# Heads' attentions: first-pass products placed by a pattern, maxima turned a step later, GpSimd storing and loading its own pieces

## What is computed

```python
q = (x_norm @ Wq + bq).reshape(B, T, H, d)     # B, T, D = 4, 512, 256; H, d = 16, 16
k = (context @ Wk + bk).reshape(B, S, H, d)    # S = 1601
v = (context @ Wv + bv).reshape(B, S, H, d)
scores = einsum('bthd,bshd->bhts', q, k) * scale      # layer 2: rotary tables on q and k; layers 2, 3: mask
attn = softmax(scores, axis=-1)
x = x + tanh(g) * (einsum('bhts,bshd->bthd', attn, v).reshape(B, T, D) @ Wo + bo)
```

## Time and the page of the profile before

| | |
|---|---|
| three runs | 3853.88, 3861.94, 3851.54 us (median 3853.88) |
| span of the profiled execution | 3829.6 us |
| median less span | 24.3 us |
| TensorE products busy | 3401.9 us (89%) |
| VectorE, ScalarE, GpSimd busy | 2159.4 (56%), 2034.7 (53%), 745.3 us (19%) |
| longest chain, shares | PE 67%, DVE 13%, DMA 8%, ACT 4%, POOL 3%, issue 3% |

### The profile page before, as it was taken

How to read it: one execution, slowest core, us unless ns; L and a number is a source line. 1 busy time by engine, 2 the same in 40 slices (tenths; PEclk the granted TensorE clock), 3 DMA queues, 4 the chain that set the end, 5 groups by cost and what they waited for, 6 DMA issues and landing times.

```text
span 3829.6 us, 52360 instructions
## 1 busy us (share of the span) xinstructions
PE 3401.9 (89%) x18396; PEld 1770.7 (46%) x18396; DVE 2159.4 (56%) x3463; ACT 2034.7 (53%) x4490; POOL 745.3 (19%) x768
## 2 busy tenths in 40 slices
PE   5899999988689989997899799989987979987997
PEld 3333333325432323332697322323326956687996
DVE  6767676736757777873402477767743033264333
ACT  2566666763236666775333266667772322244664
POOL 2211111003635331000302141210002010022332
PEclk8999999999779999998899799999998989999998
DMA  8132424105664443211874655644208521042554
GB/s 194 42 103 61 106 57 110 26 14 187 178 182 124 101 111 82 45 24 46 267 231 154 185 152 118 171 112 103 77 10 285 186 78 69 1 143 92 184 186 167
DMA packets 314686, 456.02 MB, mean 119 GB/s; under 512 B 66315, under 2 KB 234195, under 8 KB 312251
## 3 DMA queue, kind: packets, MB, share of 16 engines
q1 hardware_dynamic: 233206, 285.70, 27.5%
q0 software_dynamic: 29568, 104.65, 8.2%
q10 hardware_dynamic: 51653, 62.32, 5.8%
HBM read 292.46 MB, written 153.91 MB: 117 GB/s over the span
## 4 chain that ended last, share of the span: by engine, by line
PE 67%; DVE 13%; DMA 8%; ACT 4%; POOL 3%; issue 3%; SPq 1%; ACTq 0%; another core or an unknown queue 0%; POOLq 0%; DVEq 0%
PE pv L1325 14%; PE m L1289 11%; PE s L1311 9%; DVE mxp L1172 9%; PE h L2811 5%; PE y L2819 5%; PE h L2385 4%; PE y L2394 4%; PE y L1791 2%; PE s L1771 2%; PE s L1256 2%; DMA sums<-rc 2%; ACT e_t L1403 1%; DMA ot<-sums 1%; PE m L1333 1%
## 5 line engine op out<-in xcount | busy, mean ns | idle before, releaser
L1172 DVE TENSOR_REDUCE mxp<-m 128x1 f32<-128x802 f32 x1536 | 1447.8, 987 | 526.9 <-PE m L1289 523.2
L1403 ACT ACTIVATE e_t<-s 128x512 f32<-128x512 f32 (+1 forms) x2496 | 1340.3, 599 | 552.0 <-PE s L1311 532.9
L1289 PE MATMUL m<-kaug,qaug 97*128 97x401 bf16 x3072 | 811.6, 347 | 97.5 <-DVE mxp L1172 51.6
L1311 PE MATMUL s<-qaug,kaug 100*128 100x512 bf16 (+1 forms) x2496 | 859.4, 386 | 34.1 <-ACT e_t L1403 29.0
L1325 PE MATMUL pv<-e_t,v 128*32 128x512 f32 (+1 forms) x4992 | 670.3, 609 | 0.2
L1311 PEld LDWEIGHTS s<-qaug,kaug 100*128 100x128 bf16 (+1 forms) x2496 | 229.4, 99 | 733.8 <-ACT e_t L1403 519.6
L1289 PEld LDWEIGHTS m<-kaug,qaug 97*128 97x128 bf16 x3072 | 273.4, 99 | 506.7 <-DVE mxp L1172 265.2
L127 POOL TENSOR_TENSOR rstd<-rstd,mhalf 128x16 f32<-128x16 f32 (+2 forms) x9 | 24.2, 2690 | 1150.8 <-DVE rstd L120 1150.8
L2881 ACT ACTIVATE ez<-h,b 128x128 f32<-128x128 f32 x440 | 120.1, 388 | 159.7 <-PE h L2811 159.7
L1325 PEld LDWEIGHTS pv<-e_t,v 128*32 128x32 f32 (+1 forms) x4992 | 98.6, 108 | 214.9 <-ACT e_t L1403 161.3
L2272 DVE SCALAR_TENSOR_TENSOR y<-y,b 128x256 f32<-128x256 f32 x39 | 16.6, 425 | 303.0 <-PE y L2394 303.0
(11 more groups left out here) (377 smaller groups left out, 3616.2 us busy)
## 6 DMA issues: line engine op xcount, KB each, us to landing
w<-in_L_w POOLq DMA_DIRECT2D x78, 1024.0 KB, 5.4
w<-in_L_w SPq DMA_DIRECT2D x24, 1024.0 KB, 12.7
xregion<-zero ACTq DMA_DIRECT2D x10, 2056.0 KB, 12.2
kaug<-kparts SPq DMA_DIRECT2D x16, 1200.8 KB
kaug<-kready SPq DMA_DIRECT2D x32, 600.4 KB
kaug<-kready SPq DMA_DIRECT2D x16, 1200.8 KB
vn<-values SPq DMA_DIRECT2D x8, 1536.0 KB
values<-p_vb ACTq DMA_DIRECT2D x21, 512.0 KB
```

The costliest lines, as they stand in the source:

```text
L1172: dve.tensor_reduce(a.mxp[:, u.g % 2, half, n:n + 1], a.m_slot[u.m % 2][:].rearrange("p (a n) -> p a n", a=2)[:, :, 0:PIECE + 1], AX.XY, A ...
L1289: m = pe.matmul(slot[:, 512 * k:512 * k + PIECE + 1], a.qaug[0:R_MAX, u.g, j, P * qc:P * qc + P], a.kaug[0:R_MAX, u.g, j, k0:k0 + PIECE + ...
L1311: pe.matmul(slot[0:KW[u.k], :], a.kaug[0:R_ALL, u.g, u.j, P * u.k:P * u.k + KW[u.k]], a.qaug[0:R_ALL, u.g, u.j, :], start=True, stop=True) ...
L1403: act.activation(a.e_t[0:KW[u.k], e % 2, u.j, :], a.s_slot[u.s % 3][0:KW[u.k], :], ACT.Exp).then_inc(s_free.sem, 1)
```

## The change

Three parts. (1) A call's `max` units are placed by a table: `counts[k]` says how many step k gets, `ORDER` where they stand among the four `s2` (S) of the step. Every layer leads by 6 maxima. (2) `peak` directly follows the 32nd `max`; the `turn` is laid out at the end of the next step, ahead of that step's `pv`. (3) Pieces that GpSimd splits (all in the second and third layer but the first one, batches 1 to 3 in the first) are stored by GpSimd's own queue, and GpSimd also loads the key pieces, two pieces ahead. SyncE no longer waits for them in order; a fetch waits for the stores' semaphores.

```diff
-MAX_STEPS = 2 * HG * QC + 2
+MAXIMA = 2 * HG * QC
+LEAD = 6
+FEW = (3, 2, 3, 2, 3, 2, 3, 2, 3, 3, 1, 2, 3)
+MANY = (4, 4, 3, 4, 3, 4, 3, 4, 3, 1, 1, 2, 2)
+ORDER = ("SSSS", "SMSSS", "SMSMSS", "MSSMSSM", "MSMSMSSM")
...
-        self.lead = 8 if mask else 12
...
-    def maxima(self, g, b, begin=0, end=2 * HG * QC + 2, alone=False):
+    def maxima(self, g, b, begin=0, end=MAXIMA):
+        for i in range(begin, end):
             self.add("max", b=b, g=g, k=i)
-            if self.to_turn:
-                self.add("turn", **self.to_turn.pop())
-            yield
-        if end > 2 * HG * QC:
-            self.add("peak", b=b, g=g)
...
+            if i == MAXIMA - 1:
+                self.add("peak", b=b, g=g)
                 self.to_turn.append(dict(b=b, g=g))
             yield
+
+    def turn(self):
+        if self.to_turn:
+            self.add("turn", **self.to_turn.pop())
...
-    def attend(self, g, b, *work):
+    def attend(self, g, b, peaks, counts, *work):
         given = [0] * len(work)
         for k in range(KT):
-            for j in range(HG):
+            turning, j = bool(self.to_turn), 0
+            for it in ORDER[counts[k]]:
+                if it == "M":
+                    next(peaks, None)
+                    continue
                 self.add("s2", b=b, g=g, k=k, j=j)
                 n = HG * k + j
+                j += 1
...
+            if turning:
+                self.turn()
             if self.late:
                 self.add("pv", **self.late.pop())
...
+def head_stores_itself(a, u):
+    return u.by == "pool" and (a.ready or u.b > 0)
+
+def head_store_pool(kn, a, u):
+    pool, done, stored = kn.nc.gpsimd, kn.sema("split_pool"), kn.sema(f"pooled{u.f}", DMA)
...
+    pool.wait_ge(done.sem, done.at(u.n + 1))
+    store_parts(pool, u.kind, dst, a.split_at[u.f][2][:, :, 0:n], stored.sem)
+
+def head_load_pool(kn, a, x):
...
+    pool.dma_start(kf[:, 0:n], src).then_inc(arrived.sem, DMA)
+    for r in (0, P // 2) if rope else ():
+        pool.dma_start(kr[r:r + P // 2, 0:n], src[P // 2 - r:P - r, :]).then_inc(arrived.sem, DMA)
...
-            sp.wait_ge(split[u.by].sem, split[u.by].at(u.n + 1))
-            store_parts(sp, u.kind, dst[P * u.j:P * u.j + P, :, c0:c0 + n], a.split_at[u.f][2][:, :, 0:n], stored[u.f].sem)
+            if not head_stores_itself(a, u):
+                sp.wait_ge(split[u.by].sem, split[u.by].at(u.n + 1))
+                store_parts(sp, u.kind, dst[P * u.j:P * u.j + P, :, c0:c0 + n], a.split_at[u.f][2][:, :, 0:n], stored[u.f].sem)
...
             head_split(kn, a, u, pool, "pool")
+            if head_stores_itself(a, u):
+                head_store_pool(kn, a, u)
+            for x in splits[splits.index(u) + 2:][0:1] if a.ready else ():
+                if x.kind == "k":
+                    head_load_pool(kn, a, x)
```

More of the change, by code:

```diff
@@ L577, in lay_out @@
     def lay_out(self):
-        lead, self.late = self.lead, []
+        lead, self.late = LEAD, []
         if self.ready:
@@ L603, in lay_out @@
         v = self.project(0, (), "v")
-        for n, _ in enumerate(self.maxima(0, 0, alone=True)):
+        for n, _ in enumerate(self.maxima(0, 0)):
             if n % 2:
                 next(v, None)
+        self.turn()
         for _ in v:
@@ L634, in lay_out_ready @@
     def lay_out_ready(self):
-        lead = self.lead
+        lead = LEAD
         self.add("begin", b=0)
@@ L646, in lay_out_ready @@
         self.add("prep", k=0)
-        for _ in self.maxima(0, 0, alone=True):
+        for _ in self.maxima(0, 0):
             pass
+        self.turn()
         self.add("prep", k=1)
@@ L870, in head_sp @@
             for f in range(4):
-                if a.dmas.get(f"stored{f}"):
-                    sp.wait_ge(stored[f].sem, stored[f].at(a.dmas[f"stored{f}"]))
+                for name in (f"stored{f}", f"pooled{f}"):
+                    if a.dmas.get(name):
+                        sp.wait_ge(sig(name, DMA).sem, sig(name, DMA).at(a.dmas[name]))
             if u.b:
@@ L932, in head_ready_sp, with store @@
     piece = lambda t: t.rearrange("(c t h i) s k -> c t h i s k", c=DC, t=2, h=H // DC)
-    splits = [x for x in plan.units if x.kind in ("q", "k")]
-    held = []
-    def store():
-        if held:
-            x = held.pop()
+    def store(x):
+        if not head_stores_itself(a, x):
             (c0, n), to = (CHUNKS[x.k], keys) if x.kind == "k" else ((0, T), queries)
@@ L942, in store @@
             store_parts(sp, x.kind, to[x.b, P * x.j:P * x.j + P, :, c0:c0 + n], a.split_at[x.f][2][:, :, 0:n], stored[x.f].sem)
-            head_stored(a, x)
-    def load(x):
-        arrived, (c0, n) = sig(f"kl{x.f}", DMA), CHUNKS[x.k]
-        kf, kr, _ = a.split_at[x.f]
-        if rope and "tables_k" not in a.dmas:
-            left_values()
-            sp.dma_start(a.turn_k[:], a.rope[1]).then_inc(tables_k.sem, DMA)
-            n_of("tables_k")
-        src = kn.dram["keys"][x.b, P * x.j:P * x.j + P, c0:c0 + n]
-        if x.b in LEFT:
-            for f in range(a.p.RING):
-                kept = sig(f"p_k{f}", DMA)
-                sp.wait_ge(kept.sem, kept.at(a.p.stores[f]))
-        sp.dma_start(kf[:, 0:n], src).then_inc(arrived.sem, DMA)
-        for r in (0, P // 2) if rope else ():
-            sp.dma_start(kr[r:r + P // 2, 0:n], src[P // 2 - r:P - r, :]).then_inc(arrived.sem, DMA)
-        for _ in range(a.key_loads):
-            n_of(f"kl{x.f}")
+        head_stored(a, x)
     def left_values():
@@ L1001, in head_ready_sp @@
         elif u.kind in ("q", "k"):
-            store()
-            held.append(u)
-            after = splits[splits.index(u) + 1:][0:1]
-            for x in after:
-                if x.kind == "k":
-                    load(x)
+            store(u)
         elif u.kind == "fetch":
@@ L1010, in head_ready_sp @@
             if "q" in u.what:
-                store()
                 for f in range(2):
-                    last = max(n for (_, b, *_), (at, _, n) in a.stored_of.items() if b == u.b and at == f)
-                    sp.wait_ge(stored[f].sem, stored[f].at(last))
+                    for name in (f"stored{f}", f"pooled{f}"):
+                        of_b = [n for (_, b, *_), (at, n, _) in a.stored_of.items() if b == u.b and at == name]
+                        if of_b:
+                            sp.wait_ge(sig(name, DMA).sem, sig(name, DMA).at(max(of_b)))
             if u.b:
@@ L1084, in head_split @@
         kn.settle(eng, own, eng.tensor_tensor(src, src, a.mask[1][:, u.b:u.b + 1].to_broadcast([P, n]), ALU.mult))
-    before = a.stored_of[u.kind, u.b, u.k, u.j][1]
+    before = a.stored_of[u.kind, u.b, u.k, u.j][2]
     if before:
-        eng.wait_ge(stored.sem, stored.at(before))
+        stored = kn.sema(before[0], DMA)
+        eng.wait_ge(stored.sem, stored.at(before[1]))
     split3(kn, eng, own, kn.cst["ones"][:, 0:1].to_broadcast([P, n]), o, src, [ks[:, k, 0:n] for k in range(3)],
@@ L1094, in head_pool @@
     filled, b_made, biased = kn.sema("filled"), kn.sema("b_made"), kn.sema("biased")
+    splits = [x for x in plan.units if x.kind in ("q", "k")]
     i = pool.memset(a.fill[0:R_ALL - R_MASK, 0:S2], 1.0)
```

69 lines of the change are left out of this document (42 added, 27 removed).

## The result

| | before | now |
|---|---|---|
| median (lowest to highest) | 3855.3 us (3851.5 to 3861.9), 4 runs | 3814.8 us (3814.2 to 3818.3), 4 runs |
| ratio, 95% interval | | 0.9888 (0.9870 to 0.9907) |

A forecast was written before the change was run, and what follows sets the result against it. TensorE was taken to issue nearly without a break, with irregular calls waiting for DMAs. Terms -45 - 10 - 16 - 13 + 6 = -78 turned 3853.9 into 3776 us; forecast 3738 to 3790, 8-in-10 range 3738 to 3822.

The forecast's parts named there:

- a rival that did not happen: All attention calls: the pattern brings nothing, its 45 us go to 3, time 3818 us; chance 0.08.
- the pattern: Attention steps in all layers: new order of maxima and later turn shorten three-maxima and turn steps; -45 us left of -52.
- fewer maxima: Each layer's first call: fewer maxima for VectorE, 6 us in the first layer and 2 in each other; -10 us.
- the wait for `kaug`: First layer's call at 407.88 and two sisters: a later first maximum removes the 4.1 us wait; 5.5 x 3 = -16 us.
- SyncE not behind GpSimd: Second layer's calls at 1172.03 and 1343.60: SyncE no longer waits for GpSimd's splits, so `rc<-z` goes earlier; -13 us.
- GpSimd's new work: GpSimd's queue: 0.7 us per issue, DMAs crowding a batch's first two calls, later stores of first pieces; +6 us.
- +2: About eight third-layer calls: what steps gain before ScalarE's 3.1 us wait behind the clearing DMA becomes wait; 2 us lost.
- 2 us of its lateness would still be hidden: First layer's `kaug` calls: the fetch hanging on GpSimd's last query store could be 2 us late without cost.
- the rival that is slower than before: GpSimd's queue: issues take much longer than 0.7 us, eating the 78 us gain at 2.4 each; above 3866, chance 0.05.
- in other calls the earlier `rc<-z` was hidden and stays so: Calls other than those at 1172.03 and 1343.60: issuing `rc<-z` earlier was taken to gain nothing.
- The one of chance 0.20: First and second layers: GpSimd's queue slows others' DMAs, +21 us from late `rc<-z`, 6 of `kaug`'s 16 lost; 3803 us, chance 0.20.
- The other three rivals: Pattern brings nothing (3818, chance 0.08), slower than before (above 3866, 0.05), more than forecast (3730, 0.08).

The follow-up runs named there:

- a2: Parts one and two of the change alone (table of maxima, lead, turn), SyncE storing and loading all pieces as in the kernel before; ratio 0.9882.
- c2: Parts one and two of the change, SyncE storing, plus the clearing DMAs moved behind the sums' way back; ratio 0.9743.
- c1: The kernel before with only the third layer's clearing DMAs moved behind the sums' way back; ratio 0.9885.
- a1: The kernel before, unchanged, timed and profiled a second time; span 3864.6 us, ratio 0.9998.
- c3: The changed kernel with the clearing moved behind the sums' way back, and SyncE storing the first layer's queries and the whole third layer; ratio 0.9698.
- a3: Part three alone on the kernel before: GpSimd stores and loads the pieces it splits, with the old spread of maxima; ratio 1.0074.
- b2: The changed kernel with SyncE's load of the next values, second and third layer, issued behind the turn's DMAs; ratio 0.9858.
- b1: The changed kernel with the third layer's 2 MB clearing DMAs issued behind the sums' way back; ratio 0.9758.
- a4: The changed kernel with SyncE again storing the pieces and loading the keys in the third layer; ratio 0.9846.

## Why the prediction was right and where it failed

The time, 3815, lies in the range of 3738 to 3822 and the sign is right. The forecast itself, 3776 with 3738 to 3790, missed: it was 39 us too low, and the range holds the time only because it was drawn wide enough for two rivals. The nearest figure, 3818, belongs to a rival that did not happen (the pattern brought its 45). Against the second profile of before, call by call (the terms are by spans, and the two profiles were not taken together, so a few us of the sum can be the difference between executions):

| term | forecast | measured | from |
|---|---|---|---|
| the pattern | -45 | -45 | 1.9 (first) and 1.5 (others) a call, the third layer keeps 6 |
| fewer maxima | -10 | -8 | three first calls: -13.3, less 4.9 for the pattern |
| the wait for `kaug` | -16 | -4 | three calls: -9.8, less 5.6 |
| SyncE not behind GpSimd | -13 | -12 | two calls: -14.7, less 3.0 |
| GpSimd's new work | +6 | +21 | +8.7 second layer, +12.4 third |
| sum | -78 | -48 | by layers: -28.6, -25.5, +6.3 |

**The pattern** was right in mechanism (3.08 against 3.09 for the step). A plain call gains 1.5 and not 1.34, since the turn's step is 2.60 and not 2.72. In the third layer the "+2" for calls where "ScalarE waits 3.1 us for the sums behind the clearing DMA" was too small. In the eight calls a2 keeps 0.2 us each of the 1.5 (42.7 against 42.9): the shorter steps only reach the same landing sooner. c2 against c1 shows it: without the clearing, 15.2.

**The wait for `kaug`.** Here 12 us are missing, for two reasons. The price was too high: it took the wait of one call, 4.1 us, for all three, where a1 has 2.7, 4.8 and 2.8, and in c3, where the wait is gone, the three calls together gain 12 us beyond the pattern and not 16. The other 8 us are the step "2 us of its lateness would still be hidden". GpSimd's queue and SyncE's in the call at 395.58:

```profile
418.82 2.09 POOL L94 DMA_DIRECT2D qparts<-ks  x3 [0.30 <-POOL ks L1082]
...
423.93 0.34 SPq L931 DMA_DIRECT2D qaug<-qparts  x1
```

The last store is issued 25.3 us into the call, 3 more pass until its landing lets the fetch go, 28.4 into it. In a2, with SyncE's stores, it is 24.4. So the fetch is four microseconds late, not two; three of them are the last store, which SyncE had issued by 22.2. In the changed kernel the maximum waits again:

```profile
PE m L1320 <- DMA kaug<-kparts: 2.7, 1, 2.7
```

In the two sister calls it waits 0.9 and 3.9. c3 shows it the other way: queries back on SyncE, and all three calls at 46.

**GpSimd's work.** The price of its issues was right. The rows in the second layer, three stores and three loads behind the last of a query piece's operations:

```profile
1278.11 2.11 POOL L94 DMA_DIRECT2D qready<-ks  x3 [0.30 <-POOL ks L1082]
1280.20 0.56 POOL L850 DMA_DIRECT2D kf<-keys  x1
1280.75 1.06 POOL L852 DMA_DIRECT2D kr<-keys  x2
```

That is 0.70 a store and 0.54 a load, against the 0.70 taken, so the rival that is slower than before had no ground; the short locks that the rows spoke for stayed short (the longest of the 292 added issues took 1.0 us). What failed is the step "its DMAs crowd into the first two calls of a batch. I charge +6". The crowd cost 12.4 in the third layer (a3 alone: 24), and it is not made of GpSimd's DMAs alone. In the call at 2326.12 ScalarE's issue itself was held, with the clearing, GpSimd's pieces and SyncE's load of the values all in flight:

```profile
2342.02 0.61 ACTq L1472 DMA_DIRECT2D xregion<-zero  x1
...
2343.58 0.34 SPq L1002 DMA_DIRECT2D vn<-values  x1
...
2344.37 7.72 ACTq L1461 DMA_DIRECT2D ot<-sums  x1
```

In b2, with GpSimd's pieces and the clearing still there but the values moved, it is:

```profile
2341.04 2.07 ACTq L1465 DMA_DIRECT2D ot<-sums  x1
```

With the clearing moved instead (b1) it takes 0.55 us, and in a1 1.5. The call follows: 64.6 us, 54.8 in b2, 51.3 in b1, 55.7 in a1. So of the third layer's loss the 8.9 us of this call need both the clearing and the values ahead of `ot<-sums`; GpSimd's pieces alone do not do it. No values are loaded in the calls at 2192.59 and 2390.71: the 5.7 us of the first fall to 0.7 when SyncE stores (a4), but the 3.4 of the second stay at 2.9 there, and their cause is open. And "in other calls the earlier `rc<-z` was hidden and stays so" looked only at `rc<-z`. What SyncE also does earlier is load the values, 0.8 to 0.9 us ahead of `ot<-sums` in two calls of the second layer, which grew by 5.5 and 3.2 us (2.3 of the 5.5 come with the pattern alone) and lose 3.3 and 5.6 when the values are moved (b2). The forecast had no term for this.

**The rivals.** The one of chance 0.20, that GpSimd's queue slows the others' DMAs, is in part what happened. Its price of 27 us beside the forecast is what the table gives (12 for `kaug`, 15 for the crowd), but that the sums agree is luck: the rival had 6 and 21, of the 12 some 4 are the price set too high, and much of the 15 hangs on the load of the values. Its place was not as told either: `rc<-z` was not slowed (the reciprocal stands 11.1 us into the third layer's plain calls and 12.1 into the most crowded one), but the sums' two later DMAs and the fetch were. The rule in the Trainium skill, "DMA: Bandwidth & Descriptors", section "Queues, rings and completion order", that an engine goes round its queues, fits a `sums<-rc` that waits 15.1 us with GpSimd's queue busy and 9 to 10 without; the runs do not separate it from plain contention for the memory. The other three rivals did not come.

**What is left.** The rival's 3803 and the measured 3815 are 12 us apart. Three are the rest of the table. Some seven are the difference between 47.5 us by spans and 40.5 by medians: the second profile of before was taken in other runs than the result, and there the kernel before had a median of 3868 and not 3855. I have no other cause for it. Of what the changed kernel's third layer loses against the first profile (25.6 us), the second profile of before has 19 too. Why the first profile's execution was faster stays open.

## What to carry to other kernels

Before pricing a change, compare the profiled execution with the timed runs: here it was faster than all of them, and the eight calls that wait behind one DMA were 19 us shorter in sum than in a second profile. Read a wait in every call that it is charged to, not in one. When an engine's queue is freed, list every DMA that it now issues earlier, and what small transfer each will meet; a small transfer that others wait for should stand ahead of a bulk transfer, on its own queue and in time, and moving the bulk transfer must not put it ahead of the next small one (b2). Shorter steps are worth nothing up to a wait on a landing, so look for such waits first: the largest gain here was two lines that moved the clearing DMA.

## What the runs showed of the hardware

- An issue on ScalarE's queue took 7.7 us (8.4 in a3) 2.3 us behind a 2 MB DMA on the same queue, with GpSimd's pieces and SyncE's load of 1.5 MB in flight too. It took 2.1 with that load moved (b2), 0.55 with the 2 MB moved (b1), 1.5 in a1 and 0.53 in the median of all. ScalarE stood still for 7.1 of the 7.7 us.
- A landing 1.5 us later (11.8 to 13.3) went with 2.7 us more in a call: after TensorE's pause of 2.4 us (0.9 in the other profile) the granted clock showed 0.70 and 0.87 where it had stayed at 1.00.
- A store issued by GpSimd costs 0.70 us of its time between two pieces. From its last issue 2.4 to 3.1 us pass until SyncE's fetch behind it goes, in the three calls of the first layer; behind SyncE's own it is 1.9 to 2.6 in a1, 2.2 to 2.5 in a2 and 2.3 to 3.4 in c3, so the landing itself shows no clear difference.
